# Routed gate-up products with the weights stationary and the tile's rows streaming

## What is computed

```
scores = jax.nn.sigmoid(x @ gate_w.T) + bias
topk_w, topk_idx = jax.lax.top_k(scores, TOPK)
...
g = jnp.einsum('th,eih->eti', x, Wg)
u = jnp.einsum('th,eih->eti', x, Wu)
z = jax.nn.silu(g) * u
zw = z * cw.T[:, :, None]
out = jnp.einsum('eti,ehi->th', zw, Wd)
```

## Time and profile before

| what | value |
|---|---|
| time, median of 3 | 881.87 us (881.66 to 882.57) |
| the profiled execution's own time | 883.83 us |
| its span | 882.0 us |
| TensorE busy | 825.9 us, 94% |
| VectorE, ScalarE, GpSimd busy | 541.6, 510.7, 521.2 us |
| routed tiles | 47, one each 4.55 us |

### The profile page before, as it was taken

The page is one execution under the profiler, slowest core; times in us unless marked ns, Lnnn a source line. Parts: engine busy times, 40 slices in busy tenths (PEclk is TensorE's granted clock), DMA queues, the critical chain, the costliest instruction groups (busy, mean ns, idle before and its releaser), DMA issues.

```text
span 882.0 us, 19379 instructions
## 1 busy us (share of the span) xinstructions
PE 825.9 (94%) x6773; PEld 450.0 (51%) x6773; DVE 541.6 (61%) x1057; ACT 510.7 (58%) x1012; POOL 521.2 (59%) x442
## 2 busy tenths in 40 slices
PE   6789699999999999999999999599899999999997
PEld 2664444644645645545545545345445555555553
DVE  6897666677577577577577577498953222222236
ACT  4778677586586586586586586355323444444341
POOL 6843567877867867868868859713134444444431
PEclk9799899999999999999999999799999999999999
DMA  8055605605515515524524514724045576788943
GB/s 314 3 109 195 198 12 204 192 30 197 180 46 188 170 63 175 167 77 161 166 94 156 156 49 140 275 111 135 34 143 183 188 259 200 252 273 283 397 147 138
DMA packets 51740, 142.47 MB, mean 162 GB/s; under 512 B 6369, under 2 KB 8417, under 8 KB 47329
## 3 DMA queue, kind: packets, MB, share of 16 engines
q1 hardware_dynamic: 43568, 116.93, 39.0%
q0 software_dynamic: 7520, 24.65, 8.0%
q10 hardware_dynamic: 592, 0.08, 0.1%
HBM read 97.85 MB, written 41.68 MB: 158 GB/s over the span
## 4 chain that ended last, share of the span: by engine, by line
PE 66%; DVE 11%; POOL 11%; issue 6%; ACT 3%; DMA 2%; SPq 0%; POOLq 0%; DVEq 0%
PE ps L1566 33%; POOL reg_h L621 5%; PE ps L1990 5%; PE ps L1991 5%; PE ps L1992 5%; POOL reg_h L617 4%; PE ps L1756 2%; PE ps L1969 2%; PE ps L2013 2%; PE ps L2015 2%; PE ps L2014 2%; POOL ring_mem L566 2%; PE ps L1743 2%; PE ps L1723 1%; PE ps L2038 1%
## 5 line engine op out<-in xcount | busy, mean ns | idle before, releaser
L1566 PE MATMUL ps<-wo_hi,reg_b 128*128 128x512 f16 x448 | 144.7, 384 | 9.0 <-DVE ring_mem L1175 9.0
L621 POOL TENSOR_TENSOR reg_h<-reg_h 128x512 f16<-128x512 f32 x88 | 110.0, 1260 | 37.6 <-ACT reg_h L842 32.9
L648 POOL DMA_INDIRECT y_rows<-reg_h,to_row x47 | 48.8, 1039 | 112.4 <-ACT reg_h L1014 107.7
L580 POOL TENSOR_TENSOR ring_mem<-kv,ring_mem 128x512 f16<-128x512 f32 x64 | 82.1, 1287 | 53.6 <-ACT ring_mem L776 53.6
L1566 PE MATMUL ps<-hT_hi,wq_hi 128*128 128x512 f16 x256 | 98.1, 383 | 16.6 <-DVE ring_mem L1166 16.6
L617 POOL TENSOR_SCALAR reg_h<-reg_h 128x512 f32<-128x512 f32 x56 | 92.1, 1644 | 27.9 <-ACT reg_h L840 27.9
L1566 PE MATMUL ps<-hT_lo,wq_hi 128*128 128x512 f16 x256 | 98.0, 383 | 0.0
L1566 PE MATMUL ps<-hT_hi,wq_lo 128*128 128x512 f16 x256 | 98.0, 383 | 0.0
L1566 PE MATMUL ps<-wo_lo,reg_b 128*128 128x512 f16 x224 | 85.9, 384 | 0.0
L1566 PEld LDWEIGHTS ps<-wo_hi,reg_b 128*128 128x128 f16 x448 | 44.1, 98 | 65.6 <-issue 11.0
L1990 PE MATMUL ps<-ring_mem,reg_h 128*128 x188 | 71.3, 379 | 0.1
(11 more groups left out here) (318 smaller groups left out, 2028.1 us busy)
## 6 DMA issues: line engine op xcount, KB each, us to landing
w_split<-reg_h SPq DMA_DIRECT2D x96, 256.0 KB, 2.3
ring_mem<-w_split SPq DMA_DIRECT2D x16, 1536.0 KB
reg_h<-in_wgu SPq DMA_DIRECT2D x64, 256.0 KB, 3.5
stage<-in_wq SPq DMA_DIRECT2D x8, 1024.0 KB, 6.7
stage<-in_wo SPq DMA_DIRECT2D x8, 1024.0 KB, 4.8
reg_h<-in_wd SPq DMA_DIRECT2D x32, 256.0 KB, 3.1
wkv_st<-in_wkv SPq DMA_DIRECT2D x8, 512.0 KB, 7.3
ring_mem<-in_x_half SPq DMA_DIRECT2D x8, 256.0 KB, 5.8
```

Source lines behind the costliest of these rows:

```text
L580: pool.tensor_tensor(sq_lo[:, j // 2, 8 * th:8 * th + 8, j % 2, :], sq32[:, u % 2, :].rearrange("p (b s) -> p b s", s=S), w, ALU.subtract) ...
L621: pool.tensor_tensor(hl[:, 1, :], st, hl[:, 0, :], ALU.subtract).then_inc(pre_split, 1)
L648: pool.indirect_dma_start(y_rows, bass.IndirectOffsetOnAxis(ap=to_row[:, r - 1:r], axis=0), y[r % 2], None).then_inc(scattered[r % 2], 16)
L1566: last = pe.matmul(dst, lhsT(c), rhs(c), start=(m == 0), stop=(m == n - 1))
```

## The change

The two operands of the routed gate-up products change places. Before, 4 chunks x 3 products were made, each with the tile's rows as the stationary operand and 512 columns of weights streaming. Now a block of 128x128 weights is stationary and the 128 rows of the tile stream past it: 4 blocks of outputs (`n`, two of gate and two of up) x 4 chunks x 3 products. The result has the inner features on the partitions and the slots along them. That is the form in which `down` needs it, so `transpose_gated`, its semaphore `zT_ps` and the two PSUM banks of its results are gone. `gated_hi` and `gated_lo` read the product `tz32` in SBUF. One wait (`d_added`, 6) moves from the transposes of tile 1 to the products of tile 2.

```diff
             def gated_hi(r):
-                act.wait_ge(zT_ps, r)
-                act.activation(zT_hi[r % 2], ps[:, 2 + r % 2, 0:IC * P].rearrange("p (c s) -> p c s", c=IC),
+                act.wait_ge(z32_done, SHARED_UNITS + r)
+                act.activation(zT_hi[r % 2], tz32[r % 2].rearrange("p (c s) -> p c s", c=IC),
                                ACT.Copy).then_inc(z_hi_done, 1)
...
             def gated_up(r):
                 dve.wait_ge(silu_done, SHARED_UNITS + r)
-                if r >= 3:
-                    dve.wait_ge(zT_ps, r - 2)
...
             def gated_lo(r):
                 dve.wait_ge(z_hi_done, SHARED_UNITS + r)
-                dve.tensor_tensor(zT_lo[r % 2], ps[:, 2 + r % 2, 0:IC * P].rearrange("p (c s) -> p c s", c=IC),
+                dve.tensor_tensor(zT_lo[r % 2], tz32[r % 2].rearrange("p (c s) -> p c s", c=IC),
                                   zT_hi[r % 2], ALU.subtract).then_inc(z_split, 1)
...
+                if r == 2:
+                    pe.wait_ge(d_added, 6)
                 hi, lo = tT[r % 2][:, 0, :, :], tT[r % 2][:, 1, :, :]
-                for k in range(KC):
-                    w_hi = ring[:, bass.ds(at + 2 * BANK * k, BANK)]
-                    w_lo = ring[:, bass.ds(at + 2 * BANK * k + BANK, BANK)]
-                    pe.matmul(ps[:, r % 2, :], hi[:, k, :], w_hi, start=(k == 0), stop=False)
-                    pe.matmul(ps[:, r % 2, :], lo[:, k, :], w_hi, start=False, stop=False)
-                    last = pe.matmul(ps[:, r % 2, :], hi[:, k, :], w_lo, start=False, stop=(k == KC - 1))
+                for n in range(2 * IC):
+                    gate_t = ps[:, r % 2, n * P:(n + 1) * P]
+                    for k in range(KC):
+                        w_hi = ring[:, bass.ds(at + 2 * BANK * k + n * P, P)]
+                        w_lo = ring[:, bass.ds(at + 2 * BANK * k + BANK + n * P, P)]
+                        pe.matmul(gate_t, w_hi, hi[:, k, :], start=(k == 0), stop=False)
+                        pe.matmul(gate_t, w_hi, lo[:, k, :], start=False, stop=False)
+                        last = pe.matmul(gate_t, w_lo, hi[:, k, :], start=False, stop=(k == KC - 1))
                 last.then_inc(gu_ps, 1)
-
-            def transpose_gated(r):
-                pe.wait_ge(z32_done, SHARED_UNITS + r)
-                if r == 1:
-                    pe.wait_ge(d_added, 6)
-                for c in range(IC):
-                    last = pe.transpose(ps[:, 2 + r % 2, c * P:(c + 1) * P], tz32[r % 2][:, c * P:(c + 1) * P],
-                                        ident[:, :])
-                last.then_inc(zT_ps, 1)
...
                 if r >= 2:
                     down(r - 1, before_at)
-                transpose_gated(r)
                 before_at, now = now[0], ahead
```

More of the change, by code:

```diff
@@ L349, in decoder_kernel @@
         tT_ps, tT_hi_done, tT_lo_done = sem("tT_ps"), sem("tT_hi_done"), sem("tT_lo_done")
-        zT_ps = sem("zT_ps")
         td_ps, y_done = sem("td_ps"), sem("y_done")
```

## The result

The changed kernel takes 995.74 us (median of 5, 994.12 to 1006.61) against 882.57 (881.66 to 884.2) for the kernel before, a ratio of 1.13 with a 95% interval of 1.1255 to 1.1345. That is 113.2 us more, where 109 were forecast. The profiled execution took 1006.61 us with a span of 1004.5; it is 11 us over the median, and 9.5 of these lie ahead of the routed part (its first slot transposes start at 658.3, those of before at 648.8), in code that the change does not touch. What follows is therefore read from tile to tile.

A forecast was written before the change was run, and what follows sets the result against it. TensorE's array bounds the kernel before; its sequencer would bound the changed one at 6.9 us a tile. 46 periods give +107.6 and the end +1.3, so 881.87 + 109 = 991 us, range 910 to 1,050.

The forecast's parts named there:

- What bounds the stage: Routed tiles: TensorE's array now; after the change its sequencer, at 0.125 us a register instruction, 32 taking 4.0 us.
- The array time: Routed tile on TensorE: 48 products at 0.056 us, transposes gone; 4.43 us a tile, 0.12 less.
- rival 1: Routed stage: the array bounds after all, the sequencer's 0.125 us being an unhurried pace; faster, 876 us; 7%.
- The chain: From one tile's first sequencer wait to the next: semaphores, register instructions, table reads, hand-over, transposes and copy, wake; 6.9 us, +107.6 over 46.
- The end: Last tile, from its first wait to its own down's first product: 7.4 us against 6.1, +1.3.
- Costs taken as nothing: Routed stage: SBUF operands, dropped zT_ps waits, the moved d_added wait, gathers, scatters and ring loads add nothing.
- fetches: Sequencer's instruction fetches in the routed stage: 14 become some 30, no idle time left; 0 to +30 us, taken as next to nothing.
- 2 (cheaper issue in timed runs): TensorE's sequencer: register instructions cost 0.07 to 0.11 us in timed runs, less than under the profiler; 905 to 965; 10%.
- 3 (0.081 a product): Gate-up products: 128-column loads and matmuls go at 0.081 us, issue hidden; 5.6 us a tile, 931; 4%.
- 4 (the clock): Routed tiles: TensorE's granted clock falls to 1.2 GHz because of the hole in each tile; priced at 1,037; 17%.

The follow-up runs named there:

- static: Changed kernel with a tile's 48 gate-up products reading two fixed 128x128 weight blocks, so no register instructions in gate_up (not the layer's result): 895.2 us, ratio 1.011.

## Why the prediction was right

**What bounds the stage.** Right. The sequencer's 0.125 us for a register instruction, read off a stretch in which it hindered nobody, was its price when it did, to within 5%: 32 of them in the changed kernel take 4.2 us where 4.0 were taken. The usual step is 0.124, but four of a tile's 31 steps are longer.

**The array time.** The price of 0.056 for a 128-column product with its load was right, as static shows. What I made of it in rival 1 was not: "were the array still the bound, this would be 47 x 0.12 = 6 us less", 876. Without any register instruction it is 895.2, since the sequencer's lead is 17 small matmuls, 0.95 us, and the table reads need 1.3. That step treated the lead as unlimited. With the reads moved it is 885.77, level with the kernel before on the same chip. Rival 1 was thus not only unlikely but priced too low, by 5 to 15 us if the ratios 0.999 and 1.011 are put on 881.87.

**The chain.** Of its terms, 0.2 + 4.0 + 1.35 + 0.1 + 1.24 + 0.05 = 6.9, the tile shown above has 0.2, 4.2, 1.3 (hand-over included) and 1.25, and the next waits follow 0.1 before that copy ends, since the first of the two waits is for VectorE's: 6.8. The mean is 6.99. In 29 of the 46 steps there is neither a longer read nor a fall of the clock, and they have 6.78 to 6.99, 6.87 in the mean. The 13 with longer reads have 7.16 (16 of 94 reads took over 0.4 us; before, 2), the three with the clock at 1.2 GHz 7.2 to 7.6, and the first step, which holds other work too, 7.3. Over 46 periods the profiled execution has 321.7 us (forecast 317.4) against 210.0 before. That it comes so close is in part luck: the terms add to 6.94, not 6.9, the register instructions took 0.2 more than priced and the rest of the chain 0.3 less, and the longer reads and the falls, at nothing in the sum, put some 5 us on top.

**The end.** +1.3 was forecast. From the last slot transposes to the end it is 24.42 us in place of 23.15, so +1.27.

**Costs taken as nothing.** Dropped waits, operands in SBUF and the moved wait show nothing in the waits of the stage. The sum of the rest closes: 111.68 + 1.27 = 112.95, of 113.2 between the medians. Longer table reads were not nothing: 13 tiles x 0.29 = 3.8 us, since the reads were now on the path. On fetches the forecast counted rightly and argued wrongly. 31 instruction fetches fall in the stage, where some 30 were expected. But a tile has 36 more matmuls and 36 more loads, 72 instructions, and not "72 more matmuls and their loads". And of the 14 fetches before only 7 begin in the sequencer's idle time, not all.

**The rivals.** 2 (cheaper issue in timed runs): no sign of it, 995.74 is what the periods of the trace add up to. 3 (0.081 a product): refuted by static. 4 (the clock): the granted clock fell three times in the stage of the changed kernel, 3.4 us each, in tiles of 7.2 to 7.6 us. Against 6.87 that is 1.6 us in all, not 46. Windows around one of the falls, the clock again ahead of the last two columns:

```profile
805.00:812.00 7.00, 5.43 (x61) 3.99 (x59) 1.28 (x3) 1.88 (x4) 1.96 (x2) 1.00 0.61 209
812.20:815.50 3.30, 3.30 (x16) 1.65 (x14) 0.42 (x1) 0.67 (x2) 0.00 (x0) 0.50 0.46 189
816.00:823.00 7.00, 5.81 (x80) 4.70 (x77) 1.70 (x4) 2.22 (x6) 2.21 (x3) 1.00 0.21 75
```

**What stays open.** No version that gives the layer's result and is faster than the kernel before came out of this. In these programs each 128x128 block at a place known only at run time has its register instruction, and 32 of them with `down`'s four, the semaphores and the reads are 6.4 us against the array's 4.43. Whether a form with fewer of them exists, for one by code that is written out for each of the five places, was not tried.

## What to carry to other kernels

Count what the sequencer has to do, not only the array: an instruction that makes an address, waits or reads a table is not in the busy times, but it has a price, and cutting the same product into more pieces at run-time addresses multiplies it. Read that price from the distance between such records where they wait for nothing, and compare the sum of a loop pass with the array's. The run ahead that hides a slow read ended at 17 products here, 0.95 us at 128 columns, where 8 products of 512 columns had given 1.7: smaller matmuls shorten it in time.

## What was not expected of the hardware

- The sequencer is at most 17 matmuls of 128 columns (and their 17 loads) ahead of the array, in each of 46 tiles of static. The Trainium skill, "TensorE: Matmul & The Clock Gate", section "Architectural detail: the array is 16× 32×32, not 1× 128×128", gives TensorE's queue as 64 deep; in these rows the lead is about 34 instructions.
- A read of the table by TensorE's sequencer takes 0.30 us, but 0.4 to 1.07 us in 123 of the 287 cases in which a scatter of GpSimd's had begun 1.3 to 2.4 us earlier, and in none of the 445 in which it had begun less than 1.3 us earlier (twelve traces, without the first read of the stage). What the two share was not isolated.
- A register instruction's record is 0.046 us long, but the next one usually starts 0.124 later, whether one or two matmuls stand between them. In the changed kernel four of the 31 steps of a tile take 0.14 to 0.29, most of them 8 register instructions apart (32 instructions with their matmuls and loads), which makes the mean 0.132. What lengthens them was not isolated.
